# Experts' scatter by batch: stacked halves on 64 rows, 64-token products

## What is computed

```python
affinity = _sinkhorn(affinity_logits)              # b, expert, token
gates, idx = jax.lax.top_k(affinity, CAP)          # CAP = 2 * 256 / 16 = 32
expert_in = jnp.take_along_axis(x[:, None, :, :], idx[..., None], axis=2)
h = jax.nn.gelu(jnp.einsum('becd,edf->becf', expert_in, w1) + b1[None, :, None, :])
expert_out = jnp.einsum('becf,efd->becd', h, w2) + b2[None, :, None, :]
out = jnp.zeros_like(x)
out = out.at[jnp.arange(b)[:, None, None], idx].add(gates[..., None] * expert_out)
```

## Time and profile before

| | |
|---|---|
| median of 3 runs | 1920.71 us (1919.81 to 1920.91) |
| profiled execution, from the first to the last instruction | 1918.0 us |
| granted TensorE clock, mean over the span | 0.980 of full speed |
| TensorE busy | 1812.8 us, 95% |
| VectorE busy | 1609.1 us, 84% |
| ScalarE busy | 1564.4 us, 82% |
| GpSimd busy | 662.4 us, 35% |
| expert stage, first H products to last scatter | about 482 to 1295 us |

### The profile page before, as it was taken

One profiled execution on the slowest core, in us unless ns is written; L12 is line 12 of the kernel. 1 busy time (PEld: TensorE's weight loads), 2 busy tenths in 40 slices (PEclk: granted clock), 3 DMA queues, 4 the chain that ended last, 5 costly groups with the idle time before them and its releaser, 6 DMA issues. The chain is left out here.

```text
span 1918.0 us, 72744 instructions
## 1 busy us (share of the span) xinstructions
PE 1812.8 (95%) x28635; PEld 1311.9 (68%) x28635; DVE 1609.1 (84%) x3645; ACT 1564.4 (82%) x2773; POOL 662.4 (35%) x918
## 2 busy tenths in 40 slices
PE   6999998896999999999999999998999999999898
PEld 4777776542666666666666666766777777777677
DVE  5999987598788888888888888778999999988744
ACT  5899997575998989898989989876888888888543
POOL 4788887231000000000000000004666666655565
PEclk8999999897999999999999999999999999999899
DMA  7644545495000000000000001004665555533233
GB/s 180 130 99 93 103 94 102 139 364 187 14 11 15 13 14 11 15 13 15 10 14 14 13 12 52 2 2 107 153 169 154 144 156 147 154 69 72 64 111 121
DMA packets 312954, 160.67 MB, mean 84 GB/s; under 512 B 236558, under 2 KB 295862, under 8 KB 312374
## 3 DMA queue, kind: packets, MB, share of 16 engines
q1 hardware_dynamic: 312278, 157.95, 31.4%
q10 hardware_dynamic: 480, 0.05, 0.0%
HBM read 62.33 MB, written 36.83 MB: 52 GB/s over the span
## 5 line engine op out<-in xcount | busy, mean ns | idle before, releaser
L1793 DVE TENSOR_TENSOR h<-g,h 128x1024 f16<-128x1024 f32 x256 | 313.3, 1224 | 138.3 <-ACT h L1725 138.0
L239 PEld LDWEIGHTS psE<-ew,h 128*128 128x128 f16 x6144 | 351.2, 98 | 56.0 <-issue 40.1
L239 PE MATMUL psE<-ew,h 128*128 128x128 f16 x6144 | 365.2, 219 | 12.8 <-DVE eo L1803 6.0
L1720 ACT ACTIVATE g<-psH,eb1T 128x512 f32<-128x512 f32 x512 | 330.2, 680 | 30.9 <-PE psH L239 24.5
L814 POOL TENSOR_TENSOR Ph<-E,Ph 128x512 f16<-128x512 f32 x192 | 222.0, 1156 | 235.9 <-ACT Ph L768 235.9
L1866 POOL MEMSET rbias<- 64x384 f32 x1 | 0.4, 411 | 839.2 <-POOLq L133 839.2
L1725 ACT ACTIVATE h<-g 128x1024 f16<-128x1024 f32 x256 | 270.6, 1057 | 8.1
L720 ACT ACTIVATE vB<-psV 128x512 f16<-128x512 f32 x384 | 225.9, 589 | 51.2 <-PE psV L618 49.0
L841 DVE TENSOR_TENSOR vB<-psV,vB 128x512 f16<-128x512 f32 x384 | 248.4, 678 | 1.1 <-ACT vB L720 1.0
L618 PE MATMUL psV<-shared 96*64 96x512 f16 x1536 | 209.9, 379 | 1.5 <-DVE vB L841 1.5
L820 POOL TENSOR_TENSOR E<-E,rden 128x512 f32<-128x512 f32 x192 | 199.7, 1040 | 15.1 <-DVE rden L852 14.3
(11 more groups left out here) (308 smaller groups left out, 3417.9 us busy)
## 6 DMA issues: line engine op xcount, KB each, us to landing
keys_ahead<-shared SPq DMA_DIRECT2D x52, 512.0 KB, 4.8
shared<-keys_ahead SPq DMA_DIRECT2D x52, 512.0 KB, 3.6
rawe<-in_L_ffn_w_dram SPq DMA_DIRECT2D x32, 256.0 KB, 3.1
wb<-rw SPq DMA_DIRECT2D x64, 128.0 KB, 2.0
rows<-places SPq DMA_DIRECT2D x110, 64.0 KB, 2.5
out_dram<-x SPq DMA_DIRECT2D x7, 512.0 KB, 3.2
context_T<-shared SPq DMA_DIRECT2D x64, 48.0 KB, 2.4
PT<-Ph SPq DMA_TRANSPOSE x192, 2.8
```

The lines of the kernel that those rows point to most:

```text
L239: last = e.matmul(to, a, b, start=start and n == 0, stop=stop and n == 2, **flags)
L1720: e.activation(g32[:, ft, :], psH[:, ft, :], ACT.Gelu_apprx_tanh, bias=b1T[:, a.expert(1) * FT + ft:a.expert(1) * FT + ft + 1]).then_inc(s ...
L1793: e.tensor_tensor(h[:, 1 - par, 1, 2 * q:2 * q + 2, :], g32[:, 2 * q:2 * q + 2, :], h[:, 1 - par, 0, 2 * q:2 * q + 2, :], ALU.subtract)\
```

## The change

Five things change together.

- **Stacking.** The two halves of the gated outputs of a batch (32 slots) are laid one above the other, on 64 partitions: high half on the first 32, low half on the next 32. Eight DMAs on SP's queue do that in every step, each from 32 partitions to 32 partitions, 1 KB a partition, from `eo` to a new buffer `eoZ` (one buffer). Four of them wait for the high half, four for the low half, and all of them for the scatter of the step before.
- **Scatter.** A product now has 64 rows (both halves of one batch) and makes that batch's 64 tokens only. There are still 16 products of 128 columns, and neighbours use four different quadrants of the array.
- **Order.** The scatter comes one body later, for step j - 2, and stands between H and E. The residual moves to e = 2, the statistics to e = 3 and the even ones from 4 to 14. One body is added at the end.
- **Halves of eo.** Both are made by GpSimd now, a copy and a subtraction on 128x512 in every step, instead of ScalarE and VectorE.
- **Put and tables.** `put` is one operation on 128x512 (both inputs float16 tensors, both repeated by broadcast) instead of four on 128x128. `tok_slot` becomes float16 with 64 entries per expert and is in the new order of rows; the rows of chosen places go to `idx16` in place of a buffer of their own, and SP's loads now stand between the stacking DMAs.

```diff
@@ select_tokens, vector
-                    e.tensor_copy(gate_slot[:], psG[:])
-                    e.tensor_scalar(tok_slot[:], psI[:], block_of_p[:], None, ALU.add)
+                    e.tensor_copy(tok_slot[:], psI[:])
+                    e.tensor_copy(gate_slot[:], psG)
@@ run_experts
-            put = sb(c, "put", [P, RT, P], F16)
+            put = sb(c, "put", [P, GT, N], F16)
+            eoZ = sb(c, "eoZ", [P, GT, D], F16)
@@ sync
+                    def body(a):
+                        j = a.j
+                        if a.has(-1):
+                            wait(e, seeded["A"], j - 2)
+                            for hl, name in enumerate(("eo_hi", "eo_lo")):
+                                wait(e, s[name], j - 1)
+                                for m in range(4):
+                                    row, side = 64 * (m % 2) + 32 * hl, m // 2
+                                    e.dma_start(eoZ[row:row + 32, RT * side:RT * side + RT, :],
+                                                eo[32 * m:32 * m + 32, hl]).then_inc(s["stacked"], 16)
+                        if a.bp == 1 and a.has_tile(2):
+                            load_rows(a.t + 2)
+                        if a.e == 6 and a.G + 1 < NG:
+                            load_shares(a.G + 1)
@@ gpsimd
+                    for n in range(NE * NG):
+                        j = flat(0, 0, n)
+                        wait(e, s["gated"], j)
+                        wait(e, s["stacked"], j - 1, 128)
+                        e.tensor_copy(eo[:, 0], eo32[:]).then_inc(s["eo_hi"], 1)
+                        wait(e, s["eo_hi"], j)
+                        e.tensor_tensor(eo[:, 1], eo32[:], eo[:, 0], ALU.subtract)\
+                         .then_inc(s["eo_lo"], 1)
@@ tensor, now between H and E
-                        if a.has(-1):
-                            wait(e, s["put"], j - 1, RT)
-                            wait(e, s["eo_lo"], j - 1)
+                        if a.has(-2):
+                            wait(e, s["put"], j - 2)
+                            wait(e, s["stacked"], j - 2, 128)
...
-                                for hl in range(2):
+                                for turn in range(2):
                                     for bp in range(2):
+                                        side = (bp + turn) % 2
                                         rows = slice(64 * bp, 64 * bp + 64)
-                                        last = e.matmul(psA[:, bp, r, :], put[rows, r, :], eo[rows, hl, r, :],
+                                        to = slice(64 * side, 64 * side + 64)
+                                        last = e.matmul(psA[to, bp, r, :], put[rows, RT * side + r, :],
+                                                        eoZ[rows, RT * side + r, :], start=False,
@@ scalar
-                            if ft == 2 and a.has(-1):
-                                wait(e, s["gated"], j - 1)
-                                wait(e, seeded["A"], j - 2)
-                                e.activation(eo[:, 0], eo32[:], ACT.Copy).then_inc(s["eo_hi"], 1)
@@ vector
-                        if a.e == 1 and a.G > 0:
+                        if a.e == 2 and a.G > 0:
                             residual(a.G, -1)
-                        if a.has(-1):
-                            wait(e, seeded["A"], j - 2)
-                            for r in range(RT):
-                                e.tensor_scalar(put[:, r, :], iota[:],
-                                                tok_slot[:, a.expert(-1), a.group(-1) * RT + r:a.group(-1) * RT + r + 1],
-                                                None, ALU.is_equal).then_inc(s["put"], 1)
+                        if a.has(-2):
+                            wait(e, seeded["A"], j - 3)
+                            of_step = tok_slot[:, a.expert(-2), a.group(-2) * GT:a.group(-2) * GT + GT]
+                            e.tensor_tensor(put[:], iota[:, 0:N].unsqueeze(1).broadcast_to([P, GT, N]),
+                                            of_step.unsqueeze(2).broadcast_to([P, GT, N]), ALU.is_equal)\
+                             .then_inc(s["put"], 1)
                         h_low(0)
-                        if a.has(-1):
-                            wait(e, s["eo_hi"], j - 1)
-                            e.tensor_tensor(eo[:, 1], eo32[:], eo[:, 0], ALU.subtract)\
-                             .then_inc(s["eo_lo"], 1)
```

More of the change, by code:

```diff
@@ L1445, in _, with of_row @@
                         form_keys(e, q, psK[:, q % 4])
+                    def of_row(m):
+                        first = 64 * (m // 2) + m % 2
+                        return ident32[:, first:first + 63:2]
+                    e.wait_ge(s["kept"], 8 * GROUPS)
                     for k in range(NE):
@@ L1543, in all_steps @@
                         body(At(G, e))
+                body(At(NG - 1, NE + 1))
             with nc.Block() as block:
@@ L1547, in _, with load_rows @@
                 def _(e):
-                    def body(t):
+                    def load_rows(t):
                         wait(e, s["sel"], t - 1)
@@ L1669, in body @@
                             for r in range(RT):
-                                for hl in range(2):
+                                for turn in range(2):
                                     for bp in range(2):
+                                        side = (bp + turn) % 2
                                         rows = slice(64 * bp, 64 * bp + 64)
-                                        last = e.matmul(psA[:, bp, r, :], put[rows, r, :], eo[rows, hl, r, :],
-                                                        start=False,
-                                                        stop=a.e == NE and hl == 1, skip_group_check=True)
+                                        to = slice(64 * side, 64 * side + 64)
+                                        last = e.matmul(psA[to, bp, r, :], put[rows, RT * side + r, :],
+                                                        eoZ[rows, RT * side + r, :], start=False,
+                                                        stop=a.expert(-2) == NE - 1, skip_group_check=True)
                             last.then_inc(s["A"], 1)
+                        if a.has(0):
+                            wait(e, s["h_lo"], j, 2)
+                            wait(e, s["gated"], j - 1)
+                            for r in range(RT):
+                                for ft in range(FT):
+                                    last = matmul3(e, psE[:, r, :],
+                                                   [h[:, par, hl, ft, r * P:r * P + P] for hl in range(2)],
+                                                   [w2[:, hl, a.expert(0), ft, :] for hl in range(2)],
+                                                   r == ft == 0, ft == FT - 1, skip_group_check=True)
+                            last.then_inc(s["E"], 1)
                     all_steps(e, body)
```

69 lines of the change are left out of this document (27 added, 42 removed).

## The result

The changed kernel takes 2122.76 us (median of 4 runs, 2119.75 to 2123.85), the kernel before 1920.26 in the same session: a ratio of 1.1052 (95% interval 1.1036 to 1.1067), slower by 202 us. The forecast was 1946 us with a range of 1917 to 2005. The sign was right, the size was not: the time lies above the range, in what the prediction called the rival "SP's queue decides". The profiled execution has a span of 2122.0 us and a mean granted clock of 0.958.

The account below looks back on a forecast made before the run. TensorE was taken as the bound, busy 680 of 695 us. Bodies 9, residual 6, SP's load bodies 6, two zeros, tail 4 and token table 0.5 sum to 25 us on 1920.7: 1946 us, range 1917 to 2005.

Parts of the forecast that it names:

- The sign: Whole kernel: the change makes it slower, by 1.3%; chance of slower 0.81.
- SP's queue decides: Rival: SP's issues of 0.54 us or more, or landings near 2.0, set the body; 1965 us and above, chance 0.21.
- SP's queue: Eight stacking DMAs a body at 0.47 us: 5.9 us scatter to scatter, under 6.11, costed at nothing; at 0.64, 120.
- TensorE's own work: A body without waits goes from 6.15 to 6.11 us: quadrants in the scatter save 0.23, extra mode changes cost 0.19.
- The new wait in the alternate bodies: TensorE waits for put before the scatter: longer body 6.45 to 6.65 us, pair 12.60 to 12.76, plus 9 us.
- 6 for the residual: Once a group, the residual's two operations precede put and delay the scatter: 0.9 x 7, plus 6 us.
- GpSimd: Making both halves of eo is hidden but holds up VectorE: 0.05 us a pair of bodies, bounds 0 and 0.15.
- ScalarE's relief: ScalarE no longer makes eo's high half, so its next GELU starts earlier: minus 0.52 us in the alternate body.
- Tail: From the last E's end to the last scatter: 2.33 us becomes 6.1, plus 4 us.
- The small wait on put: Rival: put runs at 0.35 us and SP at 0.42 or less, alternate bodies 6.38; 1920 to 1926 us, chance 0.14.
- The other side: Rival: ScalarE's relief reaches VectorE early, put is always in time, every body 6.11; 1905 us, chance 0.08.
- Pairs at 1959: Rival: the scatter's products still go two at a time, 0.45 us; 1959 us, inside the forecast, chance 0.57 together.

Follow-up runs that it names:

- e2: The changed kernel without its stacking DMAs, so the experts' outputs are left out of the result; 1936.3 us.
- e4: The kernel before with one part of the change alone, both halves of eo made by GpSimd; 1895.6 us.
- e8: The kernel before with only the high half of eo made by GpSimd instead of ScalarE; 1899.3 us.
- e6: The changed kernel without stacking DMAs, put built ahead of the gating, scatter products ordered so that neighbours use only two quadrants; 1913.4 us.
- e10: The changed kernel with six stacking DMAs on SP's queue, two on GpSimd's, and two buffers of eo; 1975.5 us.
- e9: The changed kernel with six stacking DMAs issued by SP and two by GpSimd; 1987.0 us.
- e12: The changed kernel with two buffers of eo, high halves issued by SP, low halves by GpSimd, scatter behind E beside the gather; 1914.8 us.
- e13: The changed kernel with two buffers of eo, high halves issued by SP, low halves by GpSimd, put built ahead of the gating; 1957.8 us.
- e7: The changed kernel without stacking DMAs (experts' outputs left out), with the scatter behind E, beside the gather; 1892.1 us.
- e11: The changed kernel without stacking DMAs, put built ahead of the gating, all 16 scatter products on one quadrant; 1988.9 us.

## Why the prediction was wrong

**SP's queue: the step that failed.** It was costed at nothing, because "that fits under 6.11"; it measured 186 us. Two things were wrong in it. The size: I took 0.47 an issue from the earlier trace rows, while these copies take 0.59, or 0.62 from one to the next. The upper bound of 0.64 was in the text, so the value was within its bounds and judged unlikely. And the loop: I followed it from scatter to scatter, through the one stack. The tighter one passes through the one buffer of `eo`: landing, GpSimd's high half, issues, landing. GpSimd was called hidden, yet its 0.78 us is a link of it. With 0.47 this loop would have been 0.78 + 3.76 + 1.37 = 5.9 us, just inside; with 0.62 it is 7.10 in a good turn. The issue time decides between the two: the prediction's own loop also gives 5.9 with 0.47 and 7.1 with 0.62.

**Its price was also too low at the bound.** For 0.64 I had 120 us. The mean distance of E groups is 7.85 us, from 486.42 to 1483.24 in 127 steps, not 7.1 to 7.3: each slow issue (40 us in all), held high half (36) or late landing (11) is passed on whole, since nothing in the loop can catch up. The six loads of shares add 18 us, where I had 6. TensorE's lower clock is hardly part of it (4 us). A loop that is itself the bound can't be priced from a good turn; it adds up the bad ones.

**TensorE's own work: right, a little short.** Forecast 6.11 us a body; the undisturbed bodies of e2 take 6.15. The burst and its changes are nearly as foreseen: scatter to E is 0.35, so with 0.095 for the change the scatter comes out at 0.255 instead of 0.22.

**The new wait in the alternate bodies: right.** Forecast 6.65 for the longer body, 6.61 in e2, so the pair is 12.76 in both. Put took 681 ns in the change and was the releaser in e2, as said. e2 lies 16 us above the kernel before. The forecast without its copies also comes to 16: 9 for the bodies, 6 for the residual, 0.5, and 0.4 of the tail's 4. That it agrees so well is partly luck: the residual's two bodies cost 0.46 us a group more than before, 3 us in all instead of 6, while the first E comes 3.7 us later than before and not 0.5. The sign of the forecast rests on these terms and held in e2, without SP's queue.

**GpSimd: right in kind, its operations held longer than I wrote.** Low halves of h take 1455 ns on the mean in the change and 1539 in e2 against 1224 before, put 884 in e2. In e2 100 of 214 low halves are held, each beside GpSimd's subtraction, and the others take what they took before. I had only 0.05 a pair for it; the pair still came out at 12.76. But what ScalarE's relief gives was inside the sum (minus 0.52), and e4 and e8 show that it is the best part of the change.

**Tail: plus 4 forecast, plus 7 measured.** TensorE's timeline after:

```profile
1474.92 2.85 PE L236 MATMUL psE<-ew,h 128*128 128x128 f16 x48
1482.66 0.64 PE L1692 MATMUL psA<-eoZ,put 64*64 64x128 f16 x16 [4.89 <-DMA eoZ<-eo]
1483.24 3.95 PE L236 MATMUL psE<-ew,h 128*128 128x128 f16 x48
1489.67 0.42 PE L1692 MATMUL psA<-eoZ,put 64*64 64x128 f16 x16 [2.48 <-DMA eoZ<-eo]
```

A last scatter follows at 1496.7: 13.4 us from the start of the last E, against 6.5 in the kernel before (1287.9 to 1294.45 in the earlier trace rows). From that E's end it is 9.5 where I had 6.1: the last two scatters each need a whole turn of the loop.

**The rivals.** SP's queue decides: true, at a chance of 0.21, and the range cut off its upper half. The small wait on put: false, since put takes 681 ns and not 350, and the longer bodies of e2 are 6.61 and not 6.38. The other side, put always in time, was false as well; it would have been worth 15 us (1905), and the kernel with put moved ahead and no copies takes 1916. Pairs at 1959: false, since scatter to E is 0.35 us and not 0.45 and a change; nor would that order have cost anything (e6).

## What to carry to other kernels

Small DMAs in a loop are priced by the issuing queue: number of DMAs times issue time, plus a landing, plus everything between the landing and the next issue; write down every loop that passes through a tile with one buffer, not only the one to the consumer. If a loop comes near the length of the body, don't cost it at nothing, because its outliers aren't hidden: here 5.9 us were forecast under 6.11, and even e10, whose loop was put at 5.3, ended 39 us above the kernel without copies. And test the parts of a bundled change one by one: here one part alone (halves made by an idle engine) was 1.2% faster, while the whole was 10.5% slower.

## What the runs showed of the hardware, unexpected

- An SBUF to SBUF copy of 32 partitions x 1 KB costs SP 0.59 us to issue (after) and GpSimd 0.51 (e9), with the landing 1.8 and 1.7 us after the start. Single SP issues take up to 2.0 us.
- The eight copies issued within 7 us behind the first of four loads of 2.1 MB took 6.0 to 8.4 us to land (after), and 6.6 to 7.6 us on both queues in e12; no other copy took 4 us in either.
- Where GpSimd issued copies, its drain at the end of the stage lasted 11.1 to 11.2 us instead of 1.6 to 1.8, and the next stage began 7.6 to 8.1 us behind VectorE's last operation instead of 1.0 (e9, e10, e12, e13).
- Going from 64x64 to 64x128 products costs TensorE about 0.1 us, like going from 64 to 128 rows (e7).
- The order of products over the four quadrants is nearly free (0.35 against 0.37 us for 16 and the change behind them), but on a single quadrant products of 128 columns start 0.057 us apart (e11).
- GpSimd's work does not slow every VectorE operation, it holds some: in e4, 219 of 452 float16 put operations (mean 554 ns, median still 245) and none of the low halves of h (1217 against 1224); in e2, 100 of 214 low halves (mean 1539).
